# Eighteen unused products of the Hadamard matrix in each of TensorE's two longest gaps

## The chip, the cores and the metric

The program runs on one core of one Trainium2 chip. The metric is the device time of one execution in microseconds (us). A core has five engines with instruction queues of their own: TensorE (PE; its weight loads are shown apart, as PEld), VectorE (DVE), ScalarE (ACT), GpSimd (POOL) and SyncE (SP, which only issues DMAs here). They are kept in step by semaphores.

## The reference

Two transformer layers with post-norm on x of shape (2, 512, 256), all in float32. Cut to what is computed:

```python
x = _layernorm(x + _L0_attn_ref(x, Wq, Wk, Wv, Wo))
#   16 heads of 16; w = relu(q k / 4 + 0.1), causal, divided by its row sum; w v; Wo
x = _layernorm(x + _L0_ffn_ref(x, SU_ug, SU_dp, Wscale_ug, Wscale_dp, W_up, W_gate, W_down))
#   x*SU -> Hadamard transform -> gate and up (1024 wide) -> silu(gate)*up
#   -> *SU -> Hadamard transform -> down
x = _layernorm(x + _L1_attn_ref(x, w_qkv, w_out, q_norm_w, k_norm_w))
#   32 query heads and 8 key heads of 64, RMS norm, rotary positions, sliding window of 64, softmax
x = _layernorm(x + _L1_ffn_ref(x, w_gate, w_up, w_down))
```

The kernel moves the Hadamard transforms onto the weights: the small matrix `had` (128 x 128) is multiplied with them once, on PE, in `prep_ug` and `prep_down`.

## The kernel before

Everything stays on chip between the layers. The large products are done in three passes over float32 operands split in a high and a low part of type fp32r (`three`, lines 503 to 505). Other products, such as the scores and the values' sums, and all transposes take plain float32.

The order of the work is written out by hand, one list for each engine: `TENSOR_FIRST`, `SCALAR_FIRST`, `VECTOR_FIRST`, `GPSIMD_FIRST` for the attention of layer 0 and the start of its feed-forward part, `..._FILL` for its end and the start of the attention of layer 1, `..._DRAIN` for the end of that, and between them repeated passes. An engine works through its list strictly in order, and each step waits for the semaphores of what it reads and of the buffer it writes.

Six banks of PSUM form a ring. `claim` takes the next bank and waits until its last reader has emptied it; a step of `scores0` claims four banks, for four heads, before its first product. ACT turns heads 0 and 2 of the four into weights (line 945), DVE heads 1 and 3 (line 1127), and POOL sets the masked part of the diagonal block to zero (line 1395); `pv0` multiplies the weights with the values and waits, key block by key block, for that mask. `turn0` turns the result, which ACT has copied to `out_t` (line 955), and DVE divides it by its row sums (lines 1134 to 1136).

The part about 80 us in is the end of the scores of layer 0's second batch. On PE: `scores0(1,3,0)`, `prep_down(0)`, `pv0(1,2,1)`, `scores0(1,3,1)`, `turn0(1,2)`, `scores0(1,3,2)`, `prep_ug(1)`, `xt(1,0)`, `pv0(1,3,0)`, `pv0(1,3,1)`, `turn0(1,3)`, then the feed-forward part with `up(0,0)`. On DVE there stand, between the halves of the scores, the layer norm of the first batch (`ln`, line 1175) and the scaling of the down weights (line 1208):

```python
("ln", 0, 0),
("prep_down", 0), ("scores0", 1, 3, 0), ("turn0", 1, 1), ("scores0", 1, 3, 1), ("chunk", ("ug0", 1)),
("scores0", 1, 3, 2), ("turn0", 1, 2), ("prep_ug", 1), ("xt", 1, 0), ("chunk", ("ug0", 2)), ("turn0", 1, 3),
```

`chunk ug0 1` makes the low part (line 1107) that `prep_ug(1)` multiplies.

The part about 184 us in is the start of the attention of layer 1. PE has done the projections `proj1` of the first three head groups, ACT copies each from its bank (line 994), and PE turns x of the second batch (`xt(2,1)`, line 635). Then `turn1q(0,1)` (line 721) waits for the rows that DVE has normed and rotated (`roped`, lines 1289 and 1293).

At the kernel's start, while the first loads come in, `warm(5)` has PE do five products of float32 data that nobody reads (line 529).

Of the kernel before, what the change touches and what calls it, by code (L numbers as in the profile page):

```python
# [14 lines left out]
P = 128  # L15
# [45 lines left out]
RING = 6  # L61
# [23 lines left out]
def counted(k, wanted):  # L85

    return sum(1 for ch in CHUNKS[:k + 1] if wanted(ch))


def has(i):  # L90
# [52 lines left out]
    ("up", 0, 12), ("up", 0, 13), ("proj1", 0, 0), ("proj1", 0, 1), ("down", 0, 11), ("proj1", 0, 2), ("proj1", 0, 3),  # L143
    ("up", 0, 14), ("down", 0, 12), ("up", 0, 15), ("down", 0, 13), ("proj1", 1, 2), ("down", 0, 14), ("down", 0, 15),
# [150 lines left out]
def post_ln_two_layers(nc, dram, out):  # L295
    with ExitStack() as ctx:
        def sem(name):
            return ctx.enter_context(nc.semaphore(name))
# [5 lines left out]
        def keep(name, shape, dt=F32):  # L304
            return place(ctx, name, shape, dt)
# [7 lines left out]
        had = keep("hadamard", [P], F32R)  # L313
# [97 lines left out]
        ps = ctx.enter_context(nc.psum_tensor("psum", [P, 8, 512], F32))  # L411
# [3 lines left out]
        emptied_ = [sem(f"bank{i}_emptied") for i in range(8)]  # L415
# [38 lines left out]
        fills = [0] * 8  # L454
        ring_at = [0]

        def chunk_wait(eng, key):

            k = CHUNK_NO[key]
            kind, low = CHUNKS[k][2:]  # L460
            if kind != "copy":
                eng.wait_ge(ch_hi, counted(k, lambda c: c[2] != "copy"))
            eng.wait_ge(ch_lo[low], counted(k, lambda c: c[3] == low))
# [22 lines left out]
        def _(pe):  # L486
            def claim(key, bank=None):
                if bank is None:
                    bank = ring_at[0] % RING
                    ring_at[0] += 1  # L490
                job[key] = (bank, fills[bank])
                if fills[bank]:
                    pe.wait_ge(emptied_[bank], fills[bank])
                fills[bank] += 1
                for out in unmarked:
                    after_out[out] = key
                unmarked.clear()
                return ps[:, bank, :], full[bank]

            def three(o, a, b_, first, last, **kw):  # L500

                (ah_, al_), (bh_, bl_) = a, b_
                nc.tensor.matmul(o, ah_, bh_, start=first, stop=False, **kw)  # L503
                nc.tensor.matmul(o, ah_, bl_, start=False, stop=False, **kw)  # L504
                return nc.tensor.matmul(o, al_, bh_, start=False, stop=last, **kw)  # L505
# [10 lines left out]
            def x_ready(layer, b):  # L516
                if layer == 0:
                    chunk_wait(pe, ("x", b))
                else:
                    emptied(pe, *[("xt", layer, b, kb) for kb in range(KB)])  # L520

            def warm(count):
# [5 lines left out]
                for _ in range(count):  # L528
                    nc.tensor.matmul(ps[:, bank, 0:256], wt[:, 0, 0, 0:P], wt[:, 0, 0, 0:256], start=True, stop=True)

            def qk0(b, m):
                banks = {}
                if (b, m) == (0, 0):
                    pe.wait_ge(first_hi, len(HALVED))
                    pe.wait_ge(first_lo, len(HALVED))
                else:
                    x_ready(0, b)
                    chunk_wait(pe, ("w0", 0))
                by_block = [(z, kb) for kb in range(KB) for z in (1, 0)]
                by_operand = [(z, kb) for z in (1, 0) for kb in range(KB)]  # L540
                for z, kb in by_block if (b, m) == (0, 0) else by_operand:
                    if (b, m, z, kb) == (0, 0, 1, 1):
                        x_ready(0, b)
                        chunk_wait(pe, ("w0", 0))
                    if kb == 0:
                        banks[z] = claim(("qk0", b, z, m))
                    o, done = banks[z]
                    at = z * C + m * P
                    mm = three(o, (w0h[:, 0, kb, at:at + P], w0l[:, 0, kb, at:at + P]),
                               (xh[:, b, kb, :], xl[:, b, kb, :]), kb == 0, kb == KB - 1)  # L550
                    if kb == KB - 1:
                        mm.then_inc(done, 1)
# [239 lines left out]
            def attn1(k):  # L792
                for step, behind, *part in TENSOR_PASS:
                    if has(k - behind):
                        in_pass[step](k - behind, *part)

            do = dict(warm=warm, qk0=qk0, v0=v0, scores0=scores0, pv0=pv0, turn0=turn0, at0=at0, wo0=wo0, xt=xt,
                      prep_ug=prep_ug, prep_down=prep_down, up=up, down=down, attn1=attn1, **in_pass)
            for step, *args in (TENSOR_FIRST + BETWEEN + TENSOR_FILL + STEADY_STEPS
                                 + TENSOR_DRAIN + LAST):  # L800
# [744 lines left out]
```

## Time and profile before

| what | value |
|---|---|
| median of 3 runs | 517.36 us (517.0 to 517.59) |
| the profiled execution | 516.68 us, span 515.0 us |
| PE busy | 476.6 us, 93% of the span |
| DVE busy | 384.3 us, 75% |
| ACT busy | 335.3 us, 65% |
| POOL busy | 239.8 us, 47% |
| mean granted clock of TensorE | 0.989 of full speed |

The span goes from the first to the last instruction; the execution's time has some 1.7 us around it. Busy time of PE counts each matmul from its start to its modelled end, and neighbours overlap, so that the distance of the starts is the rate and not the duration of one. The chain of work is followed back from the last instruction, at each step to what released it; PE has 76% of it, DVE 11%, ACT 5%.

### The profile page before, as it was taken

To read this page: it belongs to the slowest core of one execution; us is meant where nothing else is said; L and a number is where in the kernel's file an instruction comes from. 1 tells how busy PE (TensorE), PEld (TensorE's weight loads), DVE (VectorE), ACT (ScalarE), POOL (GpSimd) and SP (SyncE) were. 2 spreads that over 40 slices of the span, in tenths; PEclk is the share of its full clock that TensorE was granted. 3 is DMA by queue.
4 is the path that set the end of the run, shared out by engine and by line. 5 is a ranking of instruction groups with operands and counts; after the bars stand their busy time and mean duration, and the time that the engine had idled before them with its cause. 6 is when DMAs were issued, how large, how long until landed. Compare 5 with 4: busy or idle time off the path is not lost.

```text
span 515.0 us, 10828 instructions
## 1 busy us (share of the span) xinstructions
PE 476.6 (93%) x3858; PEld 400.1 (78%) x3858; DVE 384.3 (75%) x678; ACT 335.3 (65%) x942; POOL 239.8 (47%) x167
## 2 busy tenths in 40 slices
PE   5899997999999967999999999998998899999995
PEld 4554554788888956789999999887987788889884
DVE  5645588778553888998989888999998975554634
ACT  4565556634634357998889898868988799333230
POOL 0477447221633476555665755656448721320001
PEclk9999998999999998999999999999999899999999
DMA  7600010033311000000000000001001301100101
GB/s 253 217 1 2 3 42 1 0 124 92 105 40 41 1 1 1 22 4 19 22 22 21 23 23 1 22 20 42 10 14 43 100 26 63 42 0 1 41 1 42
DMA packets 8900, 19.97 MB, mean 39 GB/s; under 512 B 1424, under 2 KB 2960, under 8 KB 8720
## 3 DMA queue, kind: packets, MB, share of 16 engines
q1 hardware_dynamic: 8848, 19.29, 11.8%
q8 instruction: 32, 0.52, 0.4%
q14 instruction: 20, 0.16, 0.1%
HBM read 18.23 MB, written 1.05 MB: 37 GB/s over the span
## 4 chain that ended last, share of the span: by engine, by line
PE 76%; DVE 11%; ACT 5%; issue 4%; DMA 1%; POOL 1%; SPq 0%; DVEq 0%; POOLq 0%; ACTq 0%
PE psum L503 16%; PE psum L505 15%; PE psum L504 15%; PE psum L750 5%; PE psum L578 4%; PE psum L740 4%; PE psum L762 4%; PE psum L596 4%; ACT probs L1021 3%; PE psum L721 3%; DVE minus_max L1308 2%; PE psum L730 2%; DVE roped L1293 1%; DMA raw_chunks<-in_w 1%; PE psum L713 1%
## 5 line engine op out<-in xcount | busy, mean ns | idle before, releaser
L1021 ACT ACTIVATE probs<-psum,minus_max 128x128 f32<-128x128 f32 x256 | 91.6, 396 | 15.9 <-PE psum L740 7.7
L1428 POOL TENSOR_TENSOR rope_sin_part<-qkv_rows,sin_weighted 128x640 f32<-128x640 f32 x32 | 51.4, 1628 | 48.9 <-DVE rope_cos_part L1277 42.5
L1437 POOL TENSOR_TENSOR rms_inverse<-rms_inverse,minus_half 128x20 f32<-128x20 f32 x16 | 64.6, 4039 | 1.3
L1021 ACT ACTIVATION_READ_ACCUMULATOR probs<-psum,minus_max 128x1 f32 x256 | 60.2, 235 | 0.0
L989 ACT CAST hidden_high<-hidden 128x512 fp32r<-128x512 f32 x32 | 19.9, 621 | 61.1 <-DVE hidden L1223 61.1
L1308 DVE TENSOR_REDUCE minus_max<-psum 128x4 f32<-128x512 f32 x64 | 41.9, 683 | 14.6 <-PE psum L740 13.7
L503 PE MATMUL psum<-x_t_high,ug_high_low 128*128 128x512 f32 x128 | 51.1, 400 | 0.0
L505 PE MATMUL psum<-x_t_high,ug_high_low 128*128 128x512 f32 x128 | 50.7, 396 | 0.0
L504 PE MATMUL psum<-x_t_low,ug_high_low 128*128 128x512 f32 x128 | 50.5, 395 | 0.0
L503 PE MATMUL psum<-qkv_high_low,x_t_high 128*128 128x384 f32 x128 | 46.6, 364 | 3.6 <-ACT qkv_rows L994 1.7
L1302 DVE TENSOR_TENSOR probs<-probs,prob_inverse 128x512 f32<-128x512 f32 x64 | 47.8, 747 | 2.2
L994 ACT COPY qkv_rows<-psum 128x384 f32<-128x384 f32 x64 | 31.8, 510 | 19.0 <-PE psum L505 17.8
L504 PE MATMUL psum<-qkv_high_low,x_t_high 128*128 128x384 f32 x128 | 43.3, 338 | 0.0
L505 PE MATMUL psum<-qkv_high_low,x_t_low 128*128 128x384 f32 x128 | 43.2, 338 | 0.0
L1127 DVE TENSOR_SCALAR weights_t<-psum 128x384 f32<-128x384 f32 (+1 forms) x48 | 26.6, 596 | 20.0 <-PE psum L578 20.0
L945 ACT ACTIVATE weights_t<-psum,bias_threshold 128x384 f32<-128x384 f32 (+1 forms) x48 | 27.0, 614 | 21.2 <-PE psum L578 21.2
L503 PE MATMUL psum<-wout_high,out_t_high 128*128 128x256 f32 x128 | 39.1, 305 | 0.5 <-DVE out_t_low L1077 0.5
L1226 DVE TENSOR_TENSOR hidden_low<-hidden,hidden_high 128x512 fp32r<-128x512 f32 x32 | 22.2, 694 | 22.0 <-ACT hidden_high L989 22.0
L750 PE MATMUL psum<-identity,probs 128*128 128x128 f32 x256 | 37.0, 279 | 1.2 <-ACT probs L1021 1.0
L1031 ACT COPY probs_t<-psum 128x512 f32<-128x512 f32 x64 | 37.2, 623 | 0.5 <-PE psum L750 0.5
L1395 POOL TENSOR_SCALAR_AFFINE_SELECT weights_t<-weights_t 128x512 f32<-128x512 f32 x32 | 21.0, 670 | 34.5 <-ACT weights_t L945 30.7
L503 PE MATMUL psum<-down_high_low,hidden_high 128*128 128x256 f32 x128 | 36.4, 284 | 0.5 <-issue 0.5
(156 smaller groups left out, 1381.7 us busy)
## 6 DMA issues: line engine op xcount, KB each, us to landing
raw_chunks<-in_ug SPq DMA_DIRECT2D x8, 512.0 KB, 4.0
raw_chunks<-in_wout SPq DMA_DIRECT2D x16, 256.0 KB, 2.7
raw_chunks<-in_qkv SPq DMA_DIRECT2D x8, 384.0 KB, 3.3
down_tree<-in_down SPq DMA_DIRECT2D x1, 1024.0 KB, 8.5
x_rows<-in_x_rows SPq DMA_DIRECT2D x2, 512.0 KB, 7.2
raw_chunks<-in_down SPq DMA_DIRECT2D x2, 512.0 KB, 4.4
raw_chunks<-in_x SPq DMA_DIRECT2D x2, 256.0 KB, 4.3
raw_chunks<-in_w SPq DMA_DIRECT2D x2, 256.0 KB, 4.5
```

The costliest lines, as they stand in the source:

```text
L503: nc.tensor.matmul(o, ah_, bh_, start=first, stop=False, **kw)
L504: nc.tensor.matmul(o, ah_, bl_, start=False, stop=False, **kw)
L505: return nc.tensor.matmul(o, al_, bh_, start=False, stop=last, **kw)
L750: mm = nc.tensor.transpose(o[:, q * P:(q + 1) * P], pr[:, c, q, :], ident[:])
L945: nc.scalar.activation(wt[:, hg % 2, h4, at:at + w], o[:, 0:w], ACT.Relu, bias=bias0[:]).then_inc(done, 1)
L994: nc.scalar.copy(qraw[:, k % 2, t, :], o[:, 0:GV]).then_inc(done, 1)
L1021: e = nc.scalar.activation(pr[:, c, q, :], o[:, q * P:(q + 1) * P], ACT.Exp, bias=negm[:, c, q:q + 1], accum_out=psum1[:, c, q:q + 1])
L1031: nc.scalar.copy(prt[:, c, :], o).then_inc(done, 1)
L1302: nc.vector.tensor_tensor(pr[:, c], pr[:, c], pinv[:, c, :].rearrange("p (q a) -> p q a", a=1).to_broadcast([P, 4, P]), ALU.mult).then_inc ...
L1308: nc.vector.tensor_reduce(negm[:, c, :], o.rearrange("p (q w) -> p q w", q=4), AX.X, ALU.max, negate=True).then_inc(mx_done[c], 1)
L1428: last = nc.gpsimd.tensor_tensor(ov[:, :, :, z, :], rv[:, :, :, 1 - z, :], sv[:, :, :, z, :], ALU.mult)
L1437: nc.gpsimd.tensor_tensor(r, r, half[:], ALU.pow).then_inc(rr_done, 1)
```

## The change

A new step, `idle_products(count)`, is put in two places of PE's list: 18 products between `pv0(1,2,1)` and `scores0(1,3,1)`, and 18 between `xt(2,1)` and `turn1q(0,1)`. It takes no bank: it writes the first 128 columns of the bank that the next `claim` will take, after the same wait for that bank, and the next product there starts afresh. `had` is the constant fp32r matrix of 128 x 128, both operands of each product. It raises no semaphore, and no other engine's list is changed.

```diff
@@ TENSOR_FIRST
-    ("scores0", 1, 3, 0), ("prep_down", 0), ("pv0", 1, 2, 1), ("scores0", 1, 3, 1), ("turn0", 1, 2),
+    ("scores0", 1, 3, 0), ("prep_down", 0), ("pv0", 1, 2, 1), ("idle_products", 18), ("scores0", 1, 3, 1), ("turn0", 1, 2),
@@ TENSOR_FILL
-    ("proj1", 2, 1), ("xt", 2, 1), ("turn1q", 0, 1), ("turn1k", 0), ("turn1q", 0, 0), ("proj1", 3, 1),
+    ("proj1", 2, 1), ("xt", 2, 1), ("idle_products", 18), ("turn1q", 0, 1), ("turn1k", 0), ("turn1q", 0, 0), ("proj1", 3, 1),
@@
+            def idle_products(count):
+
+                bank = ring_at[0] % RING
+                if fills[bank]:
+                    pe.wait_ge(emptied_[bank], fills[bank])
+                chunk_wait(pe, ("had", 0))
+                for _ in range(count):
+                    nc.tensor.matmul(ps[:, bank, 0:P], had[:], had[:], start=True, stop=True)
+
```

## Rows read from the trace of the kernel before

**Rows 1.** The page: busy tenths and granted clock in 40 slices of 12.9 us.
```profile
PE   5899997999999967999999999998998899999995
PEclk9999998999999998999999999999999899999999
```
**Rows 2.** Who waited for whom on PE: us in total, times, longest us.
```profile
PE psum L578 <- DVE weights_t L1127: 3.5, 2, 3.2
PE psum L721 <- DVE roped L1293: 2.9, 1, 2.9
```
**Rows 3.** Timeline about 80 us: start, duration, engine, line, names, shapes, [idle before].
```profile
77.46 1.27 ACT L945 ACTIVATE weights_t<-psum,bias_threshold 128x512 f32<-128x512 f32 x2 [5.11 <-PE psum L578]
...
78.44 1.06 PE L596 MATMUL psum<-weights_t,v_and_ones 128*32 128x256 f32 x16
...
82.73 1.13 PE L578 MATMUL psum<-q_t,k_t 32*128 32x384 f32 x8 [3.22 <-DVE weights_t L1127]
...
84.81 1.21 DVE L1107 TENSOR_TENSOR prep_low<-ug_sum_difference,prep_high 128x1024 fp32r<-128x1024 f32 x1
...
88.98 1.21 POOL L1395 TENSOR_SCALAR_AFFINE_SELECT weights_t<-weights_t 128x512 f32<-128x512 f32 x2
```
**Rows 4.** Busy time by stretch about 80 us, then granted clock, DMA share, GB/s.
```profile
82.00:84.00 2.00, 1.27 (x9) 0.56 (x10) 1.47 (x5) 1.61 (x4) 2.00 (x3) 0.83 0.00 0
84.00:86.00 2.00, 2.00 (x16) 1.52 (x19) 2.00 (x3) 0.91 (x2) 1.30 (x2) 0.50 0.00 0
86.00:88.00 2.00, 2.00 (x20) 1.56 (x13) 1.40 (x6) 1.43 (x3) 2.00 (x3) 0.81 0.00 0
```
**Rows 5.** The chain that ended last, from 82 to 92 us: start, us, what.
```profile
82.73 1.13 PE psum L578 x8
83.86 1.04 PE psum L607 x4
84.90 1.59 PE psum L578 x16
...
88.63 2.33 PE psum L596 x32
...
90.99 0.59 ACT out_t L955
```
**Rows 6.** The same chain from 33 to 37 us, at full clock.
```profile
33.60 0.86 PE psum L578 x8
...
36.09 0.87 PE psum L578 x16
```
**Rows 7.** The same chain from 71 to 75 us, at full clock.
```profile
71.60 0.12 PE psum L505
...
74.23 0.44 PE psum L607 x4
```
**Rows 8.** Timeline about 184 us.
```profile
183.12 1.04 PE L635 MATMUL psum<-identity,x_rows 128*128 128x128 f32 x8
...
183.40 0.48 ACT L994 COPY qkv_rows<-psum 128x384 f32<-128x384 f32 x1 [0.20 <-PE psum L505]
...
187.06 0.66 PE L721 MATMUL psum<-identity,roped 128*128 128x128 f32 x4 [2.90 <-DVE roped L1293]
```
**Rows 9.** Busy time by stretch from 184 to 201 us, columns as in group 4.
```profile
184.00:187.00 3.00, 0.16 (x2) 0.00 (x0) 2.94 (x9) 0.00 (x0) 2.56 (x2) 1.00 0.01 3
187.00:190.00 3.00, 2.58 (x18) 2.27 (x18) 2.94 (x8) 2.25 (x4) 3.00 (x2) 1.00 0.00 0
...
196.00:199.00 3.00, 1.32 (x19) 1.12 (x18) 2.42 (x4) 3.00 (x15) 3.00 (x2) 1.00 0.02 5
199.00:201.00 2.00, 0.92 (x5) 0.95 (x6) 1.97 (x4) 2.00 (x13) 2.00 (x2) 0.60 0.00 0
```
**Rows 10.** Groups of PE's instructions by line and shape: busy, mean ns, idle before.
```profile
L529 PE MATMUL psum<-weights_t 128*128 128x256 f32 x10 | 4.2, 597 | 1.2 <-DVE weights_t L1327 1.2
```
**Rows 11.** The chain at 216 us: products of plain float32, two halves of PE side by side.
```profile
216.24 1.02 PE psum L762 x16
```

More of the change, by code:

```diff
@@ L795, in attn1 @@
                         in_pass[step](k - behind, *part)
-            do = dict(warm=warm, qk0=qk0, v0=v0, scores0=scores0, pv0=pv0, turn0=turn0, at0=at0, wo0=wo0, xt=xt,
+            do = dict(warm=warm, idle_products=idle_products, qk0=qk0, v0=v0, scores0=scores0, pv0=pv0, turn0=turn0, at0=at0, wo0=wo0, xt=xt,
                       prep_ug=prep_ug, prep_down=prep_down, up=up, down=down, attn1=attn1, **in_pass)
```

## The prediction

> **What bounds the kernel now.** I read the slices of the page first. PE is busy nearly everywhere, and the granted clock is under its full digit in three slices, about 77 to 90, 193 to 206 and 399 to 412 us [rows 1]. Then the waits of PE: its two longest single ones are 3.2 us for DVE's weights (line 1127) and 2.9 us for DVE's rotated rows (line 1293) [rows 2]. These are the two gaps of the change. The first lies from 79.50 (78.44 + 1.06) to 82.73, the second from 184.16 (183.12 + 1.04) to 187.06 [rows 3, 8]. Neither gap is PE's own doing, and products that nobody reads cannot shorten either: DVE's list is what it was. What they can change is the clock behind the gap, so I looked at the granted clock in narrow stretches. Around the first gap it is 0.83 in 82 to 84, 0.50 in 84 to 86 and 0.81 in 86 to 88 [rows 4]. A share of 0.17, 0.50 and 0.19 of 2 us lost makes 0.34, 1.00 and 0.38, in all 1.72 us of clock lost; the engine ran at 1.2 instead of 2.4 GHz for twice that, 3.4 us, beginning about 83.3. Around the second gap the clock is 1.00 throughout, in 184 to 187 and in 187 to 190 [rows 9]. The fall near 199.4 (0.60 in 199 to 201) comes 12 us after the second gap. PE had been busy 1.32 of the 3.0 us before it, with no wait nearly as long as 2.9 [rows 9].
>
> So in the profiled execution only one of the two insertions stands ahead of a slow stretch.
>
> **What a product costs.** 128 columns of fp32r in both operands is not in the trace. The nearest row is a transposition by the identity, also 128 x 128 weights and 128 columns of four-byte data: four in 0.44, or 0.11 us each [rows 7]. An fp32r product of 256 columns takes 0.12 [rows 7], hardly more for twice the columns, which speaks for the weight load as the floor. Were it columns alone, it would be half of 0.12, 0.06 us. The upper end is plain float32: line 762 does eight products of 128 columns in 1.02 us, two side by side in the two halves of PE, or 0.255 us for a pair and at most that for one alone [rows 11]. (The warm-up products, 4.2 us for five of 256 columns, or 0.42 for 128 columns each, are the same kind at the cold start and no better as a price here [rows 10].) I take 0.11: 18 x 0.11 = 1.98 us. The ends are 18 x 0.06 = 1.1 and 18 x 0.255 = 4.6.
>
> The Trainium skill, "TensorE: Matmul & The Clock Gate", section "LDWEIGHTS (loading the stationary operand)", has a load of 128 columns at 107 ns whatever it contracts. By it the 18 products take 1.93 us, and the trace's 0.11 agrees.
>
> **The first insertion.** The products wait for the bank that the next `claim` takes. That is head 0 of `scores0(1,3,0)` (four banks, then two for `prep_down(0)`, and the ring of six is round). ACT empties it with the first of two activations, 77.46 + 0.64 = 78.10 [rows 3], before `pv0(1,2,1)` ends. They run from 79.50 to 81.5 and end 1.2 us before the scores can start at 82.73. Their cost on the path is nothing; the cover is the 3.22 us wait, and it is gone if one product takes over 3.22 / 18 = 0.18 us.
>
> What the full clock would give back, item by item, half clock against full: scores of 384 columns 1.13 against 0.86, four transposes 1.04 against 0.44, sixteen score records 1.59 against 0.87 [rows 5 to 7]; that is 0.27 + 0.60 + 0.72 = 1.59, and with the start of `prep_ug(1)` the 1.7 of the clock rows. Not all of it arrives. `prep_ug(1)` needs DVE's low part, which ends at 84.81 + 1.21 = 86.02 [rows 3]. DVE gets the scores 0.27 earlier, so 85.75. PE would then start there and not at 86.50: 0.75, plus about 0.25 for the half-speed beginning of the step, 1.0 us in hand at `pv0(1,3,0)`. Next limit: its last key blocks wait for POOL's mask, which ends at 88.98 + 1.21 = 90.19 [rows 3]. POOL's queue moves only with ACT's weights, 0.27, to 89.92. The last block is 128 of 1280 columns of the 2.33 us of `pv0`, 0.23 [rows 5], so it ends about 90.2 instead of 90.96. What is left is 0.7 to 0.8; I take 0.7. ACT's copy (0.59 at 90.99 [rows 5]), the turn and `up(0,0)` follow directly. From there to the second gap PE has nine tenths or more in every slice, 90 to 180 us [rows 1], and works off one list, so the whole later program moves by the same 0.7. Bounds: 0 if the clock falls as before, 1.7 if no queue stood in the way.
>
> **The second insertion.** The bank is that of `proj1(2,2)`, emptied by ACT ahead of the copy that starts at 183.40 [rows 8], so it is free. The products run from 184.16 to 186.1 and end 0.9 us before 187.06: cost nothing, cover gone over 2.90 / 18 = 0.16 us each. Gain in the profiled execution: nothing, as its clock did not fall. If it fell in another, the work just behind, 2.58 us busy out of 3.0 [rows 9], would run at half speed, at most 1.7 us, and probably not more than the 0.7 of the first, as DVE (2.94 of 3.0 busy) and not PE sets the pace there. The timed runs are longer than the profiled one: 517.36 against 516.68, by 0.68, what one more slow stretch would explain. I put 0.3 down to the second gap, between 0 and 0.7.
>
> **Sum.** Against its own execution: 516.68 - 0.7 = 516.0. Against the median, which is what is compared: 517.36 - 0.7 - 0.3 = 516.4 us, 0.19% less. What a measurement of this kernel can tell from no change is about 0.2%, 1.03 us: faster means under 516.3, slower over 518.4.
>
> The same page of the skill, section "What's actually happening", says that the gate's clock runs free and does not start anew with a kernel. By it the place of slow stretches differs between executions, and the 0.3 for the second gap would be nearer 0.5. No row of this single trace can show it; that 2.9 us of idle passed unpunished while a busier stretch was punished agrees.
>
> **Rivals.**
> Both gaps pay in full (20%). In most timed executions the clock falls after each, and each costs 0.7 or somewhat more: 517.36 - 1.4 to 1.9, about 515.7. For it: the 0.68 between profile and median, and two gaps of nearly equal length. Against it: full clock from 184 to 190 [rows 9].
>
> The gain is not there (17%). Either the clock falls all the same, since 18 products fill only 2 of 3.2 us, or fill 1.1 at the price of columns alone; or everything behind has moved by 0.7 and a stretch that just passed now falls, such as the one behind 187 us, where DVE and not PE sets the pace [rows 9]; one fall costs what the first gave back. 517.3. For it: the falls at 199 us and in the slice from 399 [rows 1, 9] came although PE's two longest waits are elsewhere [rows 2], and the change touches neither. Against it: in 196 to 199 PE was idle for over half of the time, while with the products the first gap is idle for under two fifths.
>
> The products are slow (13%), the rival on the other side. If fp32r with 128 columns runs like plain float32, at 0.255, 18 take 4.6 us. They end at 84.1 and 188.8, after the data are there. At the first gap the scores then end at 84.1 + 0.86 = 85.0 and not 83.86: with POOL bound to them, about 1.1 late, no slow stretch notwithstanding. At the second, 188.8 - 187.06 = 1.7 late, on the chain. 517.36 + 1.1 + 1.7 = 520.2. It decides from 0.18 us each on; at 0.21 it is 518.6. For it: the trace has no fp32r product under 256 columns. Against: the transposes at 0.11.
>
> The forecast has the remaining 50%.
>
> **How the numbers follow.** Faster: all but a tenth of the 20, and somewhat over a third of the 50, since 516.4 lies at the edge of the band: 0.38. Slower: most of the 13: 0.11. Same: 0.51. The range runs from 515.3, into the case of two gaps, to 518.3, which leaves out most of the slow products and a little at the low end.
>
> **What the changed profile would show.** Right: 36 more matmuls on PE at line 537 (or near it), 18 ending about 81.5 and 18 about 186, each 0.11 from the next; granted clock 1.00 in 82 to 88; scores of 384 columns at 0.86, the four transposes at 0.44; `up(0,0)` starting near 91.3 instead of 92.04; PE's two waits for lines 1127 and 1293 down to 1.2 and 0.9 with the same release times. Wrong: a clock under 1 in 82 to 88; starts of the scores later than 82.73; products over 0.18 apart; or `up(0,0)` earlier by 0.7 and the end not, with a new fall of the clock or a longer wait in between. The prediction fails as a whole if slow stretches elsewhere come and go by more than the one removed.

## The result and the profile after

The changed kernel takes 515.04 us (median of 7 runs, 514.45 to 516.74) against 517.59 for the kernel before; the ratio is 0.9964, 95% interval 0.9946 to 0.9982. One of the seven runs of the kernel before took 769.12 us and is left out of the ratio, which compares fast runs only. Run again beside three of the experiments it gave 0.9968 (0.9950 to 0.9986). By the ratios it is faster by about 0.35%, 1.7 to 1.9 us; the medians alone lie further apart, 2.5 and 2.0 us. 516.4 had been predicted, a gain of 1.0, with 0.38 for a gain over 0.2%. The range began at 515.3: the median of 515.04 is just under it, and the ratio on 517.36, the median that the prediction started from, gives 515.5, just inside.

The profiled execution of the changed kernel took 516.51 us, only 0.17 less than the one before, 516.68. This pair of profiles alone would have said that the change does next to nothing. Why the pair misleads is the main lesson of this case.

The page after, the same two rows as [rows 1]: the falls of the clock about 83 and 199 us are gone, and the slice from 399 to 412 still has one (at another place, as the table below shows).

```profile
PE   6899998999999987999999999989999699999995
PEclk9999999999999999999999999999999899999998
```

The timeline after about the first gap, as [rows 3]; lines below the new step have moved by nine. The 18 products (line 538) start as the last of `pv0(1,2,1)` ends. The group takes 2.23 us from the first start to the last modelled end; the starts are 0.11 us apart (36 of them take 4.24, so 18 more cost 2.01). The wait of 3.22 us is down to 1.06, and its end is set by DVE as before.

```profile
78.53 1.06 PE L605 MATMUL psum<-weights_t,v_and_ones 128*32 128x256 f32 x16
79.53 2.23 PE L538 MATMUL psum<-hadamard 128*128 128x128 f32 x18
...
82.82 0.93 PE L587 MATMUL psum<-q_t,k_t 32*128 32x384 f32 x8 [1.06 <-DVE weights_t L1136]
...
83.68 0.66 PE L616 MATMUL psum<-identity,out_t 128*128 128x128 f32 x4
...
88.88 1.22 POOL L1404 TENSOR_SCALAR_AFFINE_SELECT weights_t<-weights_t 128x512 f32<-128x512 f32 x2
...
90.65 0.58 ACT L964 COPY out_t<-psum 128x512 f32<-128x512 f32 x1 [1.59 <-PE psum L605]
...
91.70 0.48 PE L503 MATMUL psum<-x_t_high,ug_high_low 128*128 128x512 f32 x1
```

Busy time and clock in the same stretches as [rows 4]: 1.00 where it was 0.83, 0.50, 0.81.

```profile
82.00:84.00 2.00, 1.18 (x11) 0.67 (x12) 1.65 (x6) 1.76 (x4) 2.00 (x3) 1.00 0.00 0
84.00:86.00 2.00, 1.27 (x20) 0.87 (x17) 2.00 (x4) 1.24 (x3) 1.46 (x2) 1.00 0.00 0
86.00:88.00 2.00, 1.97 (x12) 1.61 (x12) 1.93 (x6) 1.82 (x5) 2.00 (x3) 1.00 0.04 8
```

At the second gap, as [rows 8], the wait falls from 2.90 to 0.94.

```profile
182.79 1.04 PE L644 MATMUL psum<-identity,x_rows 128*128 128x128 f32 x8
183.58 2.21 PE L538 MATMUL psum<-hadamard 128*128 128x128 f32 x18
186.72 0.66 PE L730 MATMUL psum<-identity,roped 128*128 128x128 f32 x4 [0.94 <-DVE roped L1302]
```

**The stretches between marks.** The total hides where time goes, since the start alone (until the scores at 82 us) differs between executions for reasons that have nothing to do with the change: 82.06 to 83.53 in the five of the kernel before, 81.75 to 84.08 in all of them. So I measured, in every profile, the distance between starts of the same instructions: A from `scores0(1,3,1)` to `up(0,0)`, B to `turn1q(0,1)`, C to `scores1(1,0)`, D to `scores1(14,0)`, E to `scores1(14,1)`. (An expectation below names `scores1(15,0)` as the end of E; the 4.5 and 6.0 us that it gives are those to `scores1(14,1)`.) B is 95.00 to 95.04, D 201.73 to 202.06 in all profiles but one B (95.92, below). What the table shows is therefore A, C and E, and beside each where the clock was at half and for how long, us from the start.

| profile | A | C | E | half clock from (us long) |
|---|---|---|---|---|
| before | 9.31 | 20.32 | 4.46 | 83.3 (3.4), 199.4 (3.4), 404.2 (3.4) |
| before, profile 2 | 11.12 | 19.07 | 4.53 | 84.0 (6.8), 189.8 (3.4), 404.8 (3.4) |
| before, profile 3 | 9.40 | 19.03 | 5.99 | 83.2 (3.4), 185.6 (6.8), 407.5 (3.4) |
| before, profile 4 | 11.09 | 19.09 | 4.46 | 84.9 (6.8), 190.7 (3.4), 405.7 (3.4) |
| before, profile 5 | 10.52 | 20.23 | 4.53 | 81.6 (6.8), 187.4 (3.4), 201.1 (3.4) |
| second gap only | 9.35 | 20.68 | 6.06 | 82.4 (3.4), 198.4 (6.8), 410.1 (3.4) |
| 9 each | 9.58 | 20.33 | 4.52 | 84.2 (3.4), 200.2 (3.4) |
| first gap only | 8.88 | 19.03 | 4.52 | 186.9 (3.4) |
| transpositions | 8.88 | 20.33 | 4.47 | 198.2 (3.4), 403.0 (3.4) |
| the change | 8.88 | 19.04 | 5.97 | 408.6 (3.4) |
| the change again | 8.88 | 19.04 | 5.98 | 408.2 (3.4) |
| 36 each | 8.91 | 18.49 | 4.44 | none |
| more places | 8.89 | 19.05 | 4.45 | 188.2 (3.4) |
| more, not gap 2 | 8.88 | 19.02 | 4.45 | 186.3 (3.4) |

(The half clock of the first 5 to 7 us, a fall about 14 us in two of them and one at the very end of each are left out.) The same length of half clock has a different price at each place: behind the first gap 0.4 to 0.7 us, or 1.6 to 2.2 when it lasts 6.8; from 185 to 191 nothing, in the six profiles that have no other fall in C, one of them with 6.8 us; about 199, 1.2 to 1.3, and 1.6 when it lasts 6.8; from 403 to 406 nothing; from 407.5 on, 1.5 to 1.6. In the first profile of the kernel before a fall stood at 404.2 and was free; in that of the change one stood at 408.6 and cost 1.5, and that ate what the absent fall at 199 had given.

The rows about 404 us show how the same length can be free or not. In the profile before, half clock covers 404.2 to 407.6. The eight transpositions take 1.79 us (1.04 in the profile of nine, at full clock), and the wait ahead of the mask product shrinks:

```profile
404.07 1.79 PE L750 MATMUL psum<-identity,probs 128*128 128x128 f32 x8
...
409.15 0.39 PE L730 MATMUL psum<-window_mask,eye_twice 64*128 64x512 bf16 x2 [0.55 <-issue]
```

In the profile of the change PE waits 2.20 us at that place at full clock, and half clock from 408.6 to 412.1 falls on products with no wait behind them, 1.98 us where the profile before has 1.09:

```profile
407.51 0.39 PE L739 MATMUL psum<-window_mask,eye_twice 64*128 64x512 bf16 x2 [2.20 <-issue]
...
409.81 1.98 PE L771 MATMUL psum<-probs_t,v_rows 128*64 128x128 f32 x16
```

The profile names no releaser for that wait. In both profiles DVE's `out_t_low` ends 0.10 us ahead of the mask product:

```profile
408.37 0.68 DVE L1077 TENSOR_TENSOR out_t_low<-psum,out_t_high 128x512 fp32r<-128x512 f32 x1
406.73 0.68 DVE L1086 TENSOR_TENSOR out_t_low<-psum,out_t_high 128x512 fp32r<-128x512 f32 x1
```

The first line is of the profile before, the second of the change. So it is likely DVE that ends the wait.

### The profile page after: what moved, and what is told of

It is laid out like the page before. It is cut to its first block, busy times and chain, and to the rows that moved or that the text cites. A ratio compares the mean times of both kernels' runs of the same rounds, so it can differ in the third digit from the quotient of the medians.

```text
span 514.8 us, 10902 instructions
## 1 busy us (share of the span) xinstructions
PE 478.4 (93%) x3894; PEld 401.6 (78%) x3894; DVE 384.4 (75%) x678; ACT 335.6 (65%) x942; POOL 239.9 (47%) x167
## 4 chain that ended last, share of the span: by engine, by line
PE 77%; DVE 10%; ACT 5%; issue 4%; DMA 1%; POOL 1%; SPq 0%; DVEq 0%; POOLq 0%; ACTq 0%
PE psum L503 17%; PE psum L505 16%; PE psum L504 15%; PE psum L759 5%; PE psum L771 4%; PE psum L587 4%; PE psum L749 4%; PE psum L605 4%; ACT probs L1030 3%; PE psum L730 2%; PE psum L739 2%; DVE minus_max L1317 2%; DMA raw_chunks<-in_w 1%; DVE roped L1302 1%; DVE square_sums L1279 1%
```

## The experiments

The first four were timed against the kernel before on one chip, the next four on another; the four further profiles of the kernel before have one execution each.

**First gap only** and **second gap only**: one of the two insertions taken out.

```diff
-    ("proj1", 2, 1), ("xt", 2, 1), ("idle_products", 18), ("turn1q", 0, 1),
+    ("proj1", 2, 1), ("xt", 2, 1), ("turn1q", 0, 1),
```

> Only the 18 products ahead of scores0(1,3,1). Clock theory, each gap pays where the clock would have fallen behind it: the profile shows full clock in 82 to 88 us, up(0,0) about 0.35 to 0.45 us earlier than before, and the time is 0.5 to 1.2 us under before, about half of the whole change. Rival, only the second gap pays in the timed runs: within 0.3 us of before. Rival, the falls only move: no gain, and as many half-clock stretches as before.

> Only the 18 products ahead of turn1q(0,1). Clock theory: the fall about 83 us is there again, none lies in 186 to 191 in any execution, and the time is 0.7 to 1.4 us under before, the rest of the whole change. Rival, the first gap does it all: within 0.3 us of before.

Measured: first gap only 0.9971 (0.9955 to 0.9986), second gap only 1.0006 (0.9991 to 1.0020). The first insertion gives the whole gain, as far as intervals of 0.8 us either way can tell; my expectation that it would be about half was wrong, and so was the 0.7 or more for the second. The profile of the first alone shows why the second has nothing to save. Its clock falls right behind the unfilled gap:

```profile
184.00:187.00 3.00, 1.34 (x13) 1.34 (x13) 2.94 (x7) 0.65 (x2) 3.00 (x2) 0.99 0.00 0
187.00:190.00 3.00, 2.85 (x10) 1.86 (x8) 3.00 (x4) 3.00 (x5) 3.00 (x2) 0.50 0.00 0
```

yet C is 19.03, and this was the fastest profiled execution of all, 513.95 us. Profile 3 of the kernel before has half clock for 6.8 us there and the same C. PE's timeline in it, the transpositions and the mask products behind them:

```profile
186.49 1.11 PE L721 MATMUL psum<-identity,roped 128*128 128x128 f32 x4 [2.91 <-DVE roped L1293]
187.40 1.06 PE L713 MATMUL psum<-identity,roped 128*128 128x128 f32 x4
188.25 1.06 PE L721 MATMUL psum<-identity,roped 128*128 128x128 f32 x4
...
191.16 0.61 PE L730 MATMUL psum<-window_mask,eye_twice 64*128 64x512 bf16 x2
196.96 0.39 PE L730 MATMUL psum<-window_mask,eye_twice 64*128 64x512 bf16 x2 [0.54 <-ACT probs L1021]
```

The transpositions take 1.1 instead of 0.6, the first mask product has no wait ahead of it where it otherwise has 1.1 us for `x_t_low`, and the second waits 0.54 for ACT. In the profile of the first gap only that second wait is 1.41:

```profile
196.14 0.39 PE L739 MATMUL psum<-window_mask,eye_twice 64*128 64x512 bf16 x2 [1.41 <-ACT probs L1030]
```

At full clock PE waits 1.1 us and then 1.5 us there, 2.6 in all behind the second gap, and a slower PE uses these waits up.

**Transpositions instead of products**: same places, same number; the wait for `had` is replaced by one for the identity.

```diff
-                    nc.tensor.matmul(ps[:, bank, 0:P], had[:], had[:], start=True, stop=True)
+                    nc.tensor.transpose(ps[:, bank, 0:P], ident[:], ident[:])
```

> The same two places, but each of the 18 is a transposition of the identity by itself in plain float32: same tile, same 0.11 us each, hence the same filling of the gaps. If any activity of PE holds the clock, it is as fast as the whole change, about 2 us under before, and the profile has full clock in 82 to 88 us. If transpositions don't count for the clock, as the page of the Trainium skill on TensorE says, the fall behind the first gap is back and the time is that of before within 0.5 us. A third reading, that the products help by something other than the clock (a filled pipeline, loaded weights): as fast as the change with the fall back in the profile.

Measured 0.9971 (0.9955 to 0.9987), mean clock of its executions 0.993 as with the products. The profile:

```profile
78.73 2.19 PE L538 MATMUL psum<-identity 128*128 128x128 f32 x18
...
82.02 0.93 PE L587 MATMUL psum<-q_t,k_t 32*128 32x384 f32 x8 [1.10 <-DVE weights_t L1136]
```

and in 82 to 88 us the clock is 1.00 throughout:

```profile
82.00:84.00 2.00, 1.69 (x16) 0.95 (x20) 1.69 (x5) 1.77 (x3) 1.73 (x2) 1.00 0.00 0
84.00:86.00 2.00, 1.53 (x19) 1.24 (x19) 2.00 (x4) 1.10 (x3) 1.74 (x2) 1.00 0.00 0
86.00:88.00 2.00, 2.00 (x18) 1.22 (x20) 1.93 (x6) 1.97 (x4) 2.00 (x2) 1.00 0.03 8
```

The third reading is out: with the gap filled the clock stayed and A was 8.88, with the products as with the transpositions. In all seven profiles with 18 or more at the first gap the clock stayed and A is 8.88 to 8.91; in all seven without (the kernel before five times, second gap only, nine) it fell. The Trainium skill, "TensorE: Matmul & The Clock Gate", "Part 4: PE-mode transpose", says that a transposition in the engine's transpose mode doesn't count as busy for the clock. The trace doesn't agree: here 18 float32 transpositions held the clock, 1.00 in 82 to 88 us, as well as 18 products. Whether they ran in that mode it doesn't say; it names them MATMUL.

**The change again.** 

> The changed kernel itself, beside the three others on one chip, to set the size of the gain: 1.4 to 2.4 us under before if the first comparison holds; 1.0 or less if it was lucky in where its slow stretches fell.

Measured 0.9968, a gain of 1.7 us; the first result was no luck. In these runs the mean clock of the kernel before was 0.985, of the first gap only 0.989, of the change 0.993. The first insertion raised the clock by 0.004 and gained 1.5 us. The second raised it by as much again, and the ratio only went from 0.9971 to 0.9968, far less than their intervals: less time at half clock isn't by itself less time.

**Nine and thirty-six products** at each place.

```diff
-("idle_products", 18)
+("idle_products", 9)        # and 36
```

> The change with 9 products at each place instead of 18, so about 1.0 us of the first gap's 3.2 is filled and 2.2 stay idle. If the clock is held only by filling most of the gap, the fall behind the first gap comes back in many executions, and the time lies between before and the change, 0.3 to 1.2 us under before. If a short interruption of the idle time is enough, it is as fast as the change, 1.6 us under before, with full clock in 82 to 88 us.

> The change with 36 products at each place: 36 x 0.11 = 4.0 us, past the end of both gaps. They would end at 83.5 and about 187.8. By the cover of the waits the scores start 0.7 us late and turn1q(0,1) 1.1 us late; both are on the chain, so the time is 1.3 to 1.8 us over the change, that is within 0.5 us of before. Rival: the first delay is caught up in the queues of DVE and POOL behind it, the second in PE's 1.1 us wait for x_t_low at 190: then 0 to 0.8 us over the change.

Nine: 0.9996 (0.9975 to 1.0017), no gain to be seen, though the interval leaves room for 1.3 us and the medians lie 0.7 apart, so that a part of the gain, as expected, isn't excluded. The mean clock is 0.987, between that of the kernel before, 0.985, and that of the first gap only, 0.989. Its profile has the fall back, with 2.07 us idle ahead of the scores, and A at 9.58:

```profile
84.00:86.00 2.00, 1.71 (x18) 1.30 (x16) 1.74 (x3) 0.65 (x2) 1.45 (x2) 0.54 0.00 0
86.00:88.00 2.00, 2.00 (x11) 1.60 (x8) 1.78 (x5) 1.71 (x4) 2.00 (x3) 0.60 0.00 0
```

Thirty-six: 0.9998 (0.9981 to 1.0015); its median of 516.21 is 0.9 over that of the change in the runs before. This profile has no fall between the start and the very end and still took 515.80 us, where the first gap only took 513.95 with a free fall (0.5 of the difference lies in the start, ahead of the first gap). The products outlast the waits:

```profile
78.97 4.24 PE L538 MATMUL psum<-hadamard 128*128 128x128 f32 x36
83.13 0.93 PE L587 MATMUL psum<-q_t,k_t 32*128 32x384 f32 x8
...
183.91 4.22 PE L538 MATMUL psum<-hadamard 128*128 128x128 f32 x36
187.96 0.62 PE L730 MATMUL psum<-identity,roped 128*128 128x128 f32 x4
```

From the products' start to the scores it is 4.16 us, with 18 of them 3.29: 0.87 late. At the second gap 4.05 against 3.14: 0.91 late, and that is the 95.92 of B. C then is 18.49 instead of 19.04, so 0.55 of the second delay is taken back by the same slack that makes a fall free there. 0.87 + 0.91 - 0.55 = 1.2; the first delay isn't caught up (A 8.91), against my rival. The 0.9 between the medians and these 1.2 lie between the two expectations, 1.3 to 1.8 and at most 0.8.

**More places**, with and without the second gap; cut to the parts that differ.

```diff
+("idle_products", 9), ("scores1", 0, 1), ("idle_products", 8, 1), ("turn1q", 1, 0)
+("idle_products", 7), ("turn1k", 14)
+("idle_products", 14, 1), ("scores1", 14, 0)
-                bank = ring_at[0] % RING
+                bank = (ring_at[0] + ahead) % RING
```

> The change, and more products where the profiles show later falls: 9 ahead of scores1(0,1) (gap of 1.5 us about 196), 8 ahead of turn1q(1,0) (1.25 us about 199), 7 ahead of turn1k(14) (1.0 us about 400) and 14 ahead of scores1(14,0) (2.2 us about 405), the second and fourth into the bank after the next, since the next is itself what is waited for. By the profiles so far a fall about 199 costs 1.3 us and one about 408 costs 1.5, and each kernel has about one of them: 0.7 to 1.3 us under the change, a mean clock over 0.996. Rival, the falls move to the next thin stretch: as fast as the change.

> The same without the 18 ahead of turn1q(0,1). If a fall about 187 costs nothing, as the profile of the kernel with the first insertion alone has it (the stretch from turn1q(0,1) to scores1(1,0) took 19.03 us with it and 19.04 without), this is as fast as the one with more places, to 0.3 us, at a lower mean clock. If the fall there matters, 0.5 us or more slower.

Measured 0.9974 (0.9957 to 0.9991) and 0.9964 (0.9945 to 0.9983). Neither profile has a fall about 199 or 408, and C and E are at their best; but the times can't be told from the change's 0.9968. The 0.7 to 1.3 us that I expected on top didn't come, nor the mean clock over 0.996: it was 0.994 and 0.992, so other executions still have falls. Leaving out the second gap's products costs nothing, as expected of a free fall. The first of the two also shows that 18 products are no guarantee. Behind the second gap, filled from 184.85 to 187, the clock fell all the same, at no cost:

```profile
184.00:187.00 3.00, 3.00 (x28) 2.88 (x26) 2.94 (x7) 0.62 (x2) 1.62 (x2) 1.00 0.01 3
187.00:190.00 3.00, 2.06 (x11) 2.00 (x11) 2.94 (x6) 0.94 (x2) 3.00 (x2) 0.69 0.00 0
```

**Four more profiles of the kernel before** (looks, in the expectations), unchanged, because A had lost only 0.43 us in its first profile while the timed gain was 1.5.

> The kernel before, profiled once more for another place of its slow stretches. Measured is the stretch from scores0(1,3,1) to up(0,0): 8.88 us at full clock in four profiles with the first insertion, 9.31 (0.43 lost) with a fall 0.6 us after its start, 9.58 (0.70 lost) with one 1.6 us after. If the whole gain of some 1.5 us lies in the fall behind the first gap, some of these looks show 1 us or more lost between scores0(1,3,1) and up(0,0). If they stay at 0.4 to 0.7, the rest of the gain is elsewhere, in falls further on that the change displaces or in chance.

> As the look before it. Also the stretch from turn1q(0,1) to scores1(1,0): 19.03 to 19.05 us with no fall, or with one that starts about 187 to 189; 20.3 with one about 199. If a fall about 187 costs nothing wherever it starts, this holds here too.

> As the two looks before it, with the stretch from scores1(14,0) to scores1(15,0) besides: 4.5 us without a fall, 6.0 with one that starts about 408.

> As the three looks before it: the sum of what the single falls cost by these stretches should give the differences between these executions, to some 0.3 us, once the start (0 to 82 us, where loads set the time) is taken out.

Three of the four had half clock behind the first gap for 6.8 us. In profile 2 it holds until past 90 us, while PE is busy:

```profile
84.00:86.00 2.00, 1.71 (x18) 1.34 (x17) 1.68 (x3) 0.60 (x2) 1.46 (x2) 0.50 0.00 0
86.00:88.00 2.00, 2.00 (x8) 1.51 (x6) 1.78 (x5) 1.74 (x3) 2.00 (x3) 0.50 0.00 0
88.00:90.00 2.00, 2.00 (x13) 1.55 (x15) 1.87 (x3) 1.48 (x3) 1.84 (x3) 0.50 0.00 0
90.00:92.00 2.00, 2.00 (x24) 0.60 (x20) 1.01 (x2) 0.38 (x1) 0.00 (x0) 0.80 0.03 8
```

Its chain has eight transpositions (line 635) at half clock, 1.71 us, which take 0.87 in the chains of the kernel before's first profile and of the change. `pv0` (line 596), with its first 1.0 us at half clock, takes 2.86 where [rows 5] has 2.33:

```profile
88.05 1.71 PE psum L635 x8
89.75 2.86 PE psum L596 x32
```

Over the five profiles of the kernel before, A loses 0.43, 2.24, 0.52, 2.21 and 1.64 against 8.88: 1.41 us in the mean. That agrees with the timed gain of the first insertion, 517.29 x 0.0029 = 1.5 us, though a mean of five values so far apart is rough. C holds at 19.03 to 19.09 in profiles 2 to 4, as expected of a free fall, and E at 4.5 and 6.0. The last expectation came true as well: against the first profile, the time from the scores to the end is longer by 0.59, 0.25, 0.57 and 1.14 us in profiles 2 to 5, and A + C + E by 0.63, 0.34, 0.54 and 1.18.

## Why the prediction was right, and where its sizes were off

- **The gaps are DVE's doing and can't be shortened by the products.** Right: both waits end with the same releaser.
- **A product costs 0.11 us and the 18 are covered.** Right: 2.23 and 2.21 us a group, starts 0.11 apart, 1.06 and 0.94 us left of the waits against 1.2 and 0.9. The scores start at 82.82 and not 82.73, but so does `pv0(1,2,1)` ahead of them, by the same 0.09. The rival of slow products, at 0.255, is out. The point from which the cover is gone was tested by the 36: late by 0.87 and 0.91.
- **The clock stays up behind the first gap.** Right in all seven profiles with 18 or more there.
- **The gain there, 0.7.** This term was mis-sized, in both directions. For the profiled execution it was 0.43: POOL's mask ended at 88.88 + 1.22 = 90.10, counted from scores that started 0.09 later, so that queue moved by 0.18 and not by 0.27, and `pv0` ended about 0.5 behind it (ACT's copy starts at 90.65), not 0.23. So `up(0,0)` starts at 91.70, not near 91.3. I had priced the last key block by its share of the columns, 128 of 1280. For the timed runs it is 1.4 to 1.5; in three of five profiles the clock stays down twice as long as in the one that I had, and A then loses 1.6 to 2.2. I took the length of a fall from a single profile, and had 1.7 as an upper bound where 2.2 occurs.
- **0.3 for the second gap.** Wrong: nothing. I reasoned from what the clock would slow, not from who waits behind it. The remark that DVE sets the pace there was nearly the right one: the waits that take up the loss are one for DVE's `x_t_low` and one for ACT. The 0.68 between median and profile, on which I put this share, fits the first gap's longer falls instead, since the first profile lost 0.43 in A and the five lose 1.41 in the mean.
- The two errors cancel in part: 0.7 + 0.3 against 1.5 + 0. That the measured time lies at the edge of the range and not well beyond it is in part luck. The rival in which both gaps pay in full was nearest in time, 515.7, and wrong in mechanism.
- **Everything behind moves by the same amount.** Right for B and D. That a stretch which just passed now falls also occurred, as in the change's profile at 408.6; but it is not tied to the change: profile 3 of the kernel before has one at 407.5. The prediction said that it fails if slow stretches elsewhere come and go by more than the one removed. In the pair of profiles they did: A is 0.43 shorter, C 1.28 shorter, E 1.51 longer. On the mean of many executions the gain is kept.

## What to carry to other kernels

Price a slow stretch of TensorE's clock by who waits behind it: the same 3.4 us cost 0 where PE had waits of its own to use up, and 1.5 where it had none. Its place and length differ from execution to execution, so take several profiles of the same kernel, compare distances between the same instructions and not totals, and time in many rounds. Filling an idle gap with unused products helps as long as they end before what they wait for; with nine the clock still fell here, and 36 outlasted the waits.

## What was not expected of the hardware

- Half clock lasting 6.8 us, twice the usual 3.4, with PE busy all the time in its second half (profile 2 of the kernel before: 2.00 of 2.00 us in 86 to 88 and in 88 to 90). What decides between the two lengths wasn't found.
- Transpositions in plain float32 hold the clock as well as fp32r products, and take as long: 18 in 2.19 us against 2.23.
- The free fall about 404 lies ahead of a wait of PE, likely for DVE: 2.20 us without the fall (profile of the change), 0.55 with it (profile before).
